# Lag attention with four context buffers, norm factors inside the context batches and squares on ScalarE; MLP pass one on three banks

## The reference

```
x = x + attention(ctx, ctx, norm(x), mask)          # 16 heads of 16
x = x + quantised_mlp(norm(x))                      # 256 -> 1024 -> 256, 8 bit
x = x + lag_attention(norm(x), ctx, ctx)
x = x + experts(norm(x))                            # shared + 2 of 8, 256 -> 1024 -> 256
```

```
q, k, v = x @ Wq + bq, ctx @ Wk + bk, ctx @ Wv + bv
corr = irfft(rfft(q) * conj(rfft(k)));  mean_value = corr.mean(heads, channels)   # [16, 256]
index = top_k(mean_value.mean(batch), k)                                        # k lags for all
w = softmax(mean_value[:, index])
out[l] = sum_k w[b, k] * v[(l + index_k) % 256];  return out @ Wo + bo
```

## Time and profile before

| what | us |
|---|---|
| median of three runs | 1219.28 |
| profiled execution | 1218.9 |
| its span, first to last instruction | 1216.7 |
| TensorE busy | 1103.1 (91%) |
| VectorE busy | 870.1 (72%) |
| ScalarE busy | 586.4 (48%) |
| GpSimd busy | 616.1 (51%) |

### The profile page before, as it was taken

How to read it: one execution, slowest core, us unless ns; L and a number is a source line. 1 busy time by engine, 2 the same in 40 slices (tenths; PEclk the granted TensorE clock), 3 DMA queues, 4 the chain that set the end, 5 groups by cost and what they waited for, 6 DMA issues and landing times. The chain is left out here.

```text
span 1216.7 us, 28250 instructions
## 1 busy us (share of the span) xinstructions
PE 1103.1 (91%) x10234; PEld 838.5 (69%) x10234; DVE 870.1 (72%) x2710; ACT 586.4 (48%) x1058; POOL 616.1 (51%) x678
## 2 busy tenths in 40 slices
PE   1699999999777988789979999999999999999996
PEld 0245544444443666667769888888898989898996
DVE  6899989998778976667845785556656666665654
ACT  1488878877654752245158333324333333343431
POOL 4887778778345949997000037722323232323233
PEclk9999999999888998999969999999999999999999
DMA  9788788888132017630487043339798989888884
GB/s 274 132 165 178 158 146 176 175 175 238 48 108 69 2 25 242 219 104 35 140 222 178 1 162 131 128 123 300 236 303 245 290 248 287 253 283 260 271 253 107
DMA packets 185116, 215.75 MB, mean 177 GB/s; under 512 B 91936, under 2 KB 167840, under 8 KB 172464
## 3 DMA queue, kind: packets, MB, share of 16 engines
q1 hardware_dynamic: 167904, 193.75, 55.4%
q0 software_dynamic: 13296, 16.92, 7.0%
q10 hardware_dynamic: 3808, 3.67, 0.9%
HBM read 143.86 MB, written 50.38 MB: 160 GB/s over the span
## 5 line engine op out<-in xcount | busy, mean ns | idle before, releaser
L2278 PE MATMUL banks<-moe_w,moe_hT 128*128 128x256 f16 x2472 | 278.7, 273 | 0.0
L2278 PEld LDWEIGHTS banks<-moe_w,moe_hT 128*128 128x128 f16 x2472 | 241.6, 98 | 27.8
L2185 ACT ACTIVATE moe_hf<-banks,moe_b 128x256 f32<-128x256 f32 (+1 forms) x440 | 178.9, 458 | 166.2 <-PE banks L2261 165.2
L2129 POOL DMA_INDIRECT out_x<-moe_y,slot_owner x71 | 115.0, 1619 | 253.9 <-DMA out_x<-moe_y,slot_owner 163.5
L749 DVE CUSTOM_DVE_ANT_0 masked<-banks,mask_bias 128x256 f32<-128x256 f32 x512 | 185.9, 420 | 24.3 <-PE banks L571 20.6
L2261 PE MATMUL banks<-moe_rT,moe_w 128*128 128x256 f16 (+1 forms) x1872 | 192.8, 263 | 0.0
L2261 PEld LDWEIGHTS banks<-moe_rT,moe_w 128*128 128x128 f16 x1872 | 169.6, 98 | 17.1
L481 ACT ACTIVATE probsT<-banks 128x1024 f32<-128x1024 f32 x128 | 130.7, 1021 | 51.2 <-PE banks L602 51.2
L2386 DVE TENSOR_TENSOR moe_hT<-moe_hf,moe_hT 128x512 f16<-128x512 f32 (+1 forms) x220 | 145.3, 661 | 7.6
L571 PE MATMUL banks<-kT,qT 48*128 48x256 f16 x512 | 92.8, 287 | 43.1 <-DMA qT<-q_split 23.2
L2114 POOL DMA_INDIRECT slots_x<-moe_xn,pos x64 | 64.8, 1013 | 118.9 <-DVE pos L2464 99.7
(11 more groups left out here) (362 smaller groups left out, 1815.5 us busy)
## 6 DMA issues: line engine op xcount, KB each, us to landing
moe_w<-moe_halves SPq DMA_DIRECT2D x80, 1024.0 KB, 5.1
moe_halves<-half_parts SPq DMA_DIRECT2D x18, 1024.0 KB, 6.0
slots_x<-empty_row SPq DMA_DIRECT2D x1, 9230.0 KB, 43.3
moe_rows<-slots_x SPq DMA_DIRECT2D x32, 260.0 KB, 6.2
half_rows<-in_L_ffn_Wfc SPq DMA_DIRECT2D x8, 1024.0 KB, 9.1
half_rows<-in_L_ffn_Wproj SPq DMA_DIRECT2D x8, 1024.0 KB, 9.0
moe_b<-in_L_ffn_bproj SPq DMA_DIRECT2D x39, 128.0 KB, 6.0
ctx_rows<-in_ctx SPq DMA_DIRECT2D x16, 256.0 KB, 3.0
```

The costliest lines, as they stand in the source:

```text
L2129: pool.indirect_dma_start(out=out_rows, out_offset=bass.IndirectOffsetOnAxis(ap=owner[:, s, t:t + 1], axis=0), in_=y[s % 2][:, t, :], in_o ...
L2185: ins = act.activation(hf[p][:, j, 0:width], src, ACT.Gelu_apprx_tanh, bias=b1[buffer][:, j:j + 1], scale=1.0 / WSCALE)
L2278: ins = pe.matmul(to, hT[p][:, x, j, t * P:(t + 1) * P], w2[buffer][:, w, j, :], start=(j == 0 and (w, x) == PARTS[0]), stop=(j == J - 1 a ...
```

## The change

- **MLP pass one.** `max_bank` goes through banks 0, 2 and 1. A pair waits for the maximum of the pair three before it. Pair 1 waits until the scales in bank 2 are copied, and the half product that is kept in bank 2 waits for the maximum of pair 28.
- **Context.** Four row buffers. SP loads batches 0 to 3 at the start; ScalarE loads batch b + 4 once b is turned. VectorE copies the cosines with the bias, ScalarE the sines.
- **Norm factors.** Statistics are taken three tiles a batch (11 batches). The first six linked steps stand at the end of batch 11, the root in ScalarE's batch 12, the other six steps in batch 13. ScalarE norms the first two batches of x ahead of the values.
- **Values.** `FIRST_VALUES` is 2 in place of 6; values 2 to 15 come after the frequencies of x.
- **Mix.** The sets of lag weights hold 2, 4, 5 and 5 batches. The addition also sums its row (`tensor_tensor_reduce`); GpSimd turns the sums of two tiles into negated means; ScalarE squares the row less its mean and sums that. VectorE's statistics go, and the factors take seven linked steps (1 + 6) in place of twelve, for the first eight tiles and for the rest.
- Semaphores are shared between steps that do not overlap.

```diff
         def max_bank(n):
-            return banks[3] if n == NC * PAIRS - 1 else banks[n % 2]
+            return banks[3] if n == NC * PAIRS - 1 else banks[(0, 2, 1)[n % 3]]
...
-                if n < 2:
-                    pe.wait_ge(m_wc, 2 * (n + 1))
+                if n == 0:
+                    pe.wait_ge(m_wc, 2)
+                elif n == 1:
+                    pe.wait_ge(m_uv, 2)
+                elif n == 2:
+                    pe.wait_ge(m_wc, 4)
                 elif n < NC * PAIRS - 1:
-                    pe.wait_ge(m_m, n - 1)
+                    pe.wait_ge(m_m, n - 2)
...
             last = banks[2]
+            pe.wait_ge(m_m, (NC - 1) * PAIRS + 1)
             first_half(last[:, 0:CW], NC - 1, 0)
...
-        FIRST_VALUES = 6
+        FIRST_VALUES = 2
+        ROWS_SEEN = 3
+        FACTORS_AT = NT // ROWS_SEEN + 2
+        MIX_SETS = ((0, 2), (2, 6), (6, 11), (11, NB))
...
-            for b in range(2):
+            for b in range(CTX):
                 sp.dma_start(ctx_in[b][:], rows[:, b, :, :]).then_inc(c_ctx[b], 16)
...
-                if b + 2 < NB:
-                    act.dma_start(ctx_in[s][:], rows[:, b + 2, :, :]).then_inc(c_ctx[s], 16)
+                if b + CTX < NB:
+                    act.dma_start(ctx_in[b % CTX][:], rows[:, b + CTX, :, :]).then_inc(c_ctx[b % CTX], 16)
...
+            def copy_sines(b):
+                act.wait_ge(c_df, b + 1)
+                act.activation(zf[:, b, 1, :], banks[3][:, 512:512 + DZ], ACT.Copy).then_inc(c_zg, 1)
...
                 keep_z(b, b % 2)
-            act.preload_act_table(ACT.Sqrt)
-            ln_scalar(act, ln, NT, g.ln_done)
-            for b in range(3):
-                keep_values(b)
+                if b >= 1:
+                    copy_sines(b - 1)
+                if b == FACTORS_AT:
+                    ln_scalar(act, ln, NT, g.ln_done)
+            copy_sines(NB - 1)
...
-            for b in range(3, FIRST_VALUES):
+            for b in range(2):
+                normalised(b, b)
+            for b in range(FIRST_VALUES):
                 keep_values(b)
-                if b < 5:
-                    normalised(b - 3, b - 3)
...
-            act.wait_ge(c_v, LAG_STEPS + g.lead + 2 + 6)
-            act.activation(ln["ln_std"][:, 0:g.lead], ln["ln_b"][:, 0:g.lead], ACT.Sqrt).then_inc(c_ex, 1)
+            stats = ln["stats"]
+            for T in range(NT):
+                act.wait_ge(c_xb, NT + T // NQ + 1)
+                if T >= 8:
+                    act.wait_ge(c_sq, T - 7)
+                act.activation(prod[T % 8][:], X[:, T, :], ACT.Square, bias=stats[:, T, MINUS_MEAN:MINUS_MEAN + 1], scale=1.0,
+                               accum_out=stats[:, T, SQUARES:SQUARES + 1]).then_inc(c_sq, 1)
+                if T == g.lead + 5:
+                    act.wait_ge(c_v, LAG_STEPS + 1)
+                    act.activation(ln["ln_std"][:, 0:g.lead], ln["ln_b"][:, 0:g.lead], ACT.Sqrt).then_inc(c_ex, 1)
...
+            for b in range(NB):
+                two = slice(NQ * b, NQ * (b + 1))
+                pool.wait_ge(c_xa, NQ * (b + 1))
+                pool.tensor_scalar(stats[:, two, MINUS_MEAN], stats[:, two, SUM], -1.0 / D, None, ALU.mult).then_inc(c_xb, 1)
...
-                for t in range(NQ):
-                    v.bn_stats(ln["stats"][:, NQ * b + t, :], X[:, NQ * b + t, :]).then_inc(ln["s_lnv"], 1)
+                for T in range(ROWS_SEEN * b, min(ROWS_SEEN * (b + 1), NT)):
+                    v.bn_stats(ln["stats"][:, T, :], X[:, T, :]).then_inc(ln["s_lnv"], 1)
+                if b == FACTORS_AT - 1:
+                    variance()
+                if b == FACTORS_AT + 1:
+                    factors()
             copy_zf(NB - 1)
-            ln_vector(v, ln, NT, D, g.ln_done)
+            v.wait_ge(c_zg, NB)
...
-                v.tensor_tensor(X[:, T, :], X[:, T, :], banks[T % 4][:, 0:D], ALU.add).then_inc(c_xa, 1)
-                if T >= 1:
-                    see(T - 1)
-                if T == g.lead + 2:
+                v.tensor_tensor_reduce(X[:, T, :], X[:, T, :], banks[T % 4][:, 0:D], 1.0, 0.0, ALU.add, ALU.add, stats[:, T, SUM:SUM + 1]).then_inc(c_xa, 1)
+                if T == g.lead + 5:
                     lead_begin()
-                if T == g.lead + 6:
+                if T == g.lead + 8:
                     lead_end()
-            see(NT - 1)
```

More of the change, by code:

```diff
@@ L82, in link, with variance, factors @@
         v.wait_ge(m["s_lnv"], done)
[L84 to L99, removed]
+    def variance():
+        v.wait_ge(m["s_lnv"], done)
+        link(v.tensor_tensor(ln_a[:], stats[:, :, 1], stats[:, :, 4], ALU.subtract))
+        link(v.tensor_tensor(nmr[:], stats[:, :, 1], stats[:, :, 4], ALU.add))
+        link(v.tensor_tensor(ln_b[:], stats[:, :, 2], stats[:, :, 5], ALU.add))
+        link(v.scalar_tensor_tensor(ln_a[:], ln_a[:], 0.25, ln_a[:], ALU.mult, ALU.mult))
+        link(v.scalar_tensor_tensor(ln_b[:], ln_b[:], 1.0 / D, ln_a[:], ALU.mult, ALU.add))
+        link(v.tensor_scalar(ln_b[:], ln_b[:], EPS, None, ALU.add))
+    def factors():
+        v.wait_ge(m["s_lns"], done_before[1] + 1)
+        link(v.reciprocal(rstd[:], m["ln_std"][:]))
+        link(v.tensor_tensor(ln_a[:], rstd[:], rstd[:], ALU.mult))
+        link(v.tensor_tensor(ln_a[:], ln_a[:], ln_b[:], ALU.mult))
+        link(v.tensor_scalar(ln_a[:], ln_a[:], -0.5, 1.5, ALU.mult, ALU.add))
+        link(v.tensor_tensor(rstd[:], rstd[:], ln_a[:], ALU.mult))
+        link(v.scalar_tensor_tensor(nmr[:], nmr[:], -0.5, rstd[:], ALU.mult, ALU.mult))
+    return variance, factors
 def see_rows(v, g, X, lo, hi):
@@ L1378, in autocorrelation @@
     BIG = 1e30
+    CTX = 4
     with ExitStack() as ctx:
@@ L1393, in autocorrelation @@
         bias_bc = sb("bias_bc", [P, D])
-        zf_bias = sb("zf_bias", [P, NQ, DZ])
-        ctx_in = [sb(f"c_rows{s}", [P, NQ, D]) for s in range(2)]
+        zf_bias = sb("zf_bias", [P, DZ])
+        ctx_in = [sb(f"c_rows{s}", [P, NQ, D]) for s in range(CTX)]
         z = [sb(f"z{s}", [P, 2, NQ, DZ], F16) for s in range(2)]
@@ L1418, in autocorrelation @@
         lag_dram = nc.dram_tensor("lag_weights", [NB, 2 * 2 * S], F16).ap()
-        c_ctx = [sem(f"c_ctx_in{s}") for s in range(2)]
+        c_ctx = [sem(f"c_ctx_in{s}") for s in range(CTX)]
         c_set = sem("c_constants_set")
@@ L1448, in autocorrelation @@
         LAG_STEPS = 13
-        c_xb = sem("c_x_bias_added")
+        c_xb = sem("c_x_bias_added_then_minus_mean_ready")
+        c_sq = sem("c_squares_summed")
+        SUM, MINUS_MEAN, SQUARES = range(3)
         block = ctx.enter_context(nc.Block())
@@ L1628, in z_frequencies @@
                     pe.wait_ge(c_zf, b)
+                    pe.wait_ge(c_zg, b)
                 for j in range(NQ):
@@ L1687, in _ @@
                 values(b)
-            pe.wait_ge(c_vl, NB)
+            pe.wait_ge(c_zl, NB + NB)
             for b in range(NB):
-                if b % (NB // 4) == 0:
-                    pe.wait_ge(c_mx[b // (NB // 4)], 32)
+                for q, (lo, hi) in enumerate(MIX_SETS):
+                    if b == lo:
+                        pe.wait_ge(c_mx[q], 32)
                 for l in range(NQ):
@@ L1797, in _ @@
             twice = lag_e[:].rearrange("b s -> b () s").to_broadcast([NB, 2, S])
-            v.tensor_scalar(lag_w[:, 0], twice, first[:, 0:1], None, ALU.mult).then_inc(c_lw, 1)
-            v.wait_ge(c_lw, 1)
-            v.scalar_tensor_tensor(lag_w[:, 1], twice, first[:, 0:1], lag_w[:, 0], ALU.mult, ALU.subtract).then_inc(c_lw, 1)
+            v.tensor_scalar(lag_w[:, 0], twice, first[:, 0:1], None, ALU.mult).then_inc(c_fr, 1)
+            v.wait_ge(c_fr, 4)
+            v.scalar_tensor_tensor(lag_w[:, 1], twice, first[:, 0:1], lag_w[:, 0], ALU.mult, ALU.subtract).then_inc(c_fr, 1)
             for b in range(FIRST_VALUES + 2, NB):
```

92 lines of the change are left out of this document (38 added, 54 removed).

## The result

The kernel after takes 1186.28 us (median of 4 runs, 1183.74 to 1189.28); the kernel before, beside it, 1219.76 (4 runs). The ratio is 0.9732, 95% interval 0.9699 to 0.9765. The profiled execution of after took 1185.54 (span 1183.6). The forecast was 1193.6, range 1185 to 1202: faster, as foretold, and by 33.5 us in place of 25.3.

A forecast was written before the change was run, and what follows sets the result against it. TensorE was taken to bound the kernel, with gains only in its waits ahead of the expert stage. Terms -6.8 - 15.5 - 5.8 + 4.6 - 1.8 = -25.3 took 1218.9 us to 1193.6, range 1185 to 1202.

The forecast's parts named there:

- split pairs: Sign in pass one of the MLP: split pairs follow each other every 2.1 us instead of 2.66.
- transposes 15: Sign in the context batches: transposes 15 some 42 us after transposes 1, against 58.0 before.
- x 2.6 behind the context: Sign for the factors: x's first product comes 2.6 us behind the last frequency of the context.
- the mixing ended by ScalarE: Sign in the mixing: ScalarE ends the stage, 23 us after the mix starts; term -1.8 us (-3 to +2).
- the clock at 1.00 throughout: Sign: the granted clock does not leave 1.00 between context and mix's end for more than a few us.
- The lock: Lag choice beside GpSimd: some ten VectorE steps held by shared ports, 0.46 us each; +4.6 us (0 to +7).
- up to 6.9 in all: Upper bound in the lag choice: each of ten VectorE steps waits for what is left of a bias addition.
- Pass one: MLP pass one on three banks: about 4.2 us a chunk, 0.7 at the entry; -6.8 us (-4 to -9).
- Batches and mixing: Context batches: -15.5 us from four buffers, +1.0 for the factors' chain inside them; mixing: -1.8 us, TensorE setting the pace.
- Four buffers issue 12.4 us ahead: Context loads: issued 12.4 us ahead, over the longest landing, so late loads go; -15.5 us (-8 to -16).
- The term of -12.1: Between context batches and x's frequencies: two values stand there instead of six and the factors' chain, 12.1 us earlier.
- Rival 3: Better than forecast: VectorE fills its slack in pass one (-2), the lock costs nothing; 1188 us, chance 0.15.

The follow-up runs named there:

- no_bias_sums: The kernel after without GpSimd's 32 bias additions, the output bias left out of x; 1185.93 us, ratio to before 0.9732.
- after_again: The kernel after, unchanged, run once more beside another kernel; 1187.58 us, ratio to before 0.9738.
- three_banks_alone: The kernel before with only pass one of the MLP taking its products through three banks in turn; 1212.13 us, ratio to before 0.9942.
- six_values_ahead: The kernel after with six values ahead of the frequencies of x in place of two; 1192.34 us, ratio to before 0.9788.
- factors_behind: The kernel after with the chain of norm factors back behind the context batches, two values still ahead; 1194.86 us, ratio to before 0.9801.
- two_buffers: The kernel after with two context buffers in place of four; 1207.24 us, ratio to before 0.9877.
- additions_earlier: The kernel after with GpSimd's last four cuts behind its 32 bias additions, the last store behind the lag weights' loads; 1202.00 us, ratio to before 0.9851.

## Why the prediction was right, and where it was off

The mechanisms were right, and the signs that it named came: split pairs 2.06 apart on the mean (22.6 / 11; named 2.1), one wait for a load, batches of 3.09 us but for the two with the chain, transposes 15 42.9 us after transposes 1 (named 42), x 2.6 behind the context, the mixing ended by ScalarE, its last sum 23.0 and the next stage's first operation 23.3 after the start (named 23 and 23.2), the clock at 1.00 throughout. The sum was 7.8 too small, in these terms:

- *This execution*, 4.1: the attention and what lies around the stages was 2.5 shorter than in the profiled execution of before, the expert stage 1.6. In the other profiles the expert stage took 599.2 to 603.0 (no_bias_sums left out, whose x differs) and the MLP began at 327.1 to 331.2, where none changes the attention; before stood at 602.6 and 330.4, on the long side of both. I made the sum against one execution and put 0 there. I take these to be the execution and not the change, but that is not shown: the medians of after and before beside each other differ by 33.5, and by 31.2 for after_again, 2.2 to 4.5 more than the 29.0 of the five stages. A part may be late loads, which do not cost before's kernel the same each time (batches and way to x, both untouched, took 1.9 more in three_banks_alone); the cause stays open.
- *The lock*, 2.3: "Term: +4.6". Six steps were held, not ten, by 0.39 on the mean (forecast 0.46); the choice grew by 7.6, of which the four values are 5.2. More than the size was wrong: the upper bound, "up to 6.9 in all", stood on the step "each of the ten steps would wait for what is left of a bias addition". A step can wait for the whole queue of additions, 11.8 and 13.0 us here. The first step in after (532.80) comes 4 us ahead of the additions (536.82), but that alone does not spare the kernel: its four later steps stand beside the same additions and were let in after one at most, as were all steps of six_values_ahead and factors_behind. Why is open. The term's range should have been open above. Where the Trainium skill says that the second of two engines waits until the first is done (SBUF — State Buffer, "Who interferes with whom"), the steps of 0.55 to 1.10 agree, and the 12.99 does not: eighteen operations were done in that time.
- *Pass one*, 0.9: a chunk takes 4.11 on the mean, not 4.2, as VectorE uses nearly all of the slack that I gave it in part; that is 0.6, and the entry gave 0.3 more than I put.
- *Batches and mixing*, 0.5: -14.7 against -14.5, -2.1 against -1.8.

"Four buffers issue 12.4 us ahead" was more than needed: with 9.3 (three buffers) the batches were no longer. The term of -12.1 was right by its total: 5.2 is the four values, 4.4 the chain, 1.5 the waits for low halves that six values in a row bring with them; the last 1.0 no run takes apart (the clock was 0.88 there before and 1.00 after). Rival 3 (1188) came nearest, by its direction: VectorE fills its slack (0.9 of the 2 given), the lock costs half.

## What to carry to other kernels

Ask of each VectorE step that slides beside GpSimd not only how long GpSimd's operation is, but whether a queue without pauses stands behind it; a wait between its operations (with the loop written out) cost GpSimd 0.15 us each here and spared a stop of 12. Compare how far ahead loads are issued with their landings: here 6.2 us ahead lost 13.8 and 9.3 ahead lost nothing, with longest landings of 9.5 and 9.8, and what late loads cost differs from run to run. A sum of stages is compared with other stages cut at the same instructions: that separates a change of 2 us which the whole time, with a spread of 2 to 3, doesn't show.

## What the runs showed of the hardware

- A VectorE operation on 128x16 numbers with 0.23 us of work stood 11.82 and 12.99 us while GpSimd did 17 and 18 additions of 0.68 without a gap, and ended 0.03 and 0.6 us behind the last of them. Beside the same additions in six_values_ahead four such steps were let in after one addition each (0.70, 0.66, 0.64, 0.66), and in factors_behind too (0.47, 0.65, 0.64, 0.66). The steps kept out came 10.1 and 9.5 us behind the first addition and these 2.8 and 2.3, but a later step of six_values_ahead was let in 11.8 us behind it (0.70). What decides between the two stays open.
- Of the three executions behind two_buffers' time two took 1207.2 and 1208.9 and one 1197.2, about the cost of such a stop lower; that this one was let in is argued, not shown.
- Behind a wait of TensorE of about 2 us the clock fell or did not, in the same kernel (products of 1.47 us in all at 2.4 GHz, 2.74 at 1.2). Behind 3 us too: the products ran at the lower level behind 3.03 (six_values_ahead), at the full one behind 3.08 (three_banks_alone, granted 1.00 from 525.3 to 530.0) and 3.21 (before, 1.00 from 489.3 to 493.3). Behind 4.12 and 4.91 (before), 4.20 (factors_behind), 12.75 (two_buffers) and 14.38 (additions_earlier) they began at the lower level.
